# Window attention: v comes out with two windows' tokens on the partitions, and four copies deal the heads to the halves

## The reference

```
L0: window attention, windows of 8x8 tokens (4 per sample), 12 heads of 8 channels
    qkv = x_w @ qkv_w.T + qkv_b;  softmax(q k^T * scale + bias) v;  proj
L1: shifted window attention, the same windows after a roll by 4, 12 heads of 32 channels
    q, k, v = split(x_s @ w_qkv);  softmax(q k^T * scale + pos + masks) v;  @ w_out + b_out
L2: depthwise 3x3 convolution and a pointwise one, with weights rounded to -1, 0, 1
L3: attention with rounded activations ("spikes"), without softmax
```

## Time and profile before

| | us |
|---|---|
| median of 3 runs | 438.77 (437.97 to 439.72) |
| profiled execution | 439.99 |
| its span, first to last instruction | 438.1 |
| PE busy | 382.5 |
| DVE busy | 320.0 |
| ACT busy | 246.3 |
| POOL busy | 197.1 |
| v products (L736), PE busy, L1 and L0 | 26.4 and 11.1 |
| v copies (L923), DVE busy | 46.8 |

### The profile page before, as it was taken

The page is one execution under the profiler, slowest core; times in us unless marked ns, Lnnn a source line. Parts: engine busy times, 40 slices in busy tenths (PEclk is TensorE's granted clock), DMA queues, the critical chain, the costliest instruction groups (busy, mean ns, idle before and its releaser), DMA issues.

```text
span 438.1 us, 13521 instructions
## 1 busy us (share of the span) xinstructions
PE 382.5 (87%) x4971; PEld 282.5 (64%) x4971; DVE 320.0 (73%) x730; ACT 246.3 (56%) x554; POOL 197.1 (45%) x319
## 2 busy tenths in 40 slices
PE   0178599999999999999999999999999999858773
PEld 0168377888888787777777777777777533325441
DVE  0488288777787867878777777777878679965783
ACT  0010366878778675665666666666566455457871
POOL 8202056675666754445444444444544352442341
PEclk9999999999999999999999999999999999997996
DMA  8900000000000000000000000000000000000111
GB/s 290 166 9 1 0 4 1 4 0 0 0 0 0 3 2 3 2 1 1 2 3 1 0 0 0 0 0 1 1 2 3 1 0 0 1 0 18 39 37 54
DMA packets 8520, 7.15 MB, mean 16 GB/s; under 512 B 5058, under 2 KB 8130, under 8 KB 8354
## 3 DMA queue, kind: packets, MB, share of 16 engines
q1 hardware_dynamic: 3984, 5.26, 4.1%
q10 hardware_dynamic: 4498, 1.38, 1.8%
HBM read 5.06 MB, written 1.57 MB: 15 GB/s over the span
## 4 chain that ended last, share of the span: by engine, by line
PE 63%; DVE 16%; issue 9%; POOL 4%; DMA 3%; ACT 3%; DVEq 0%; POOLq 0%; ACTq 0%
PE bank L726 12%; PE bank L760 12%; PE bank L789 11%; PE bank L769 9%; PE bank L736 6%; DVE conv L1238 5%; PE bank L833 4%; PE bank L818 3%; DMA table<-in_L_conv_rpb_table 3%; POOL y_out L1437 2%; PE bank L555 2%; DVE stats L584 2%; DVE row_max L961 2%; PE bank L835 1%; PE bank L1346 1%
## 5 line engine op out<-in xcount | busy, mean ns | idle before, releaser
L999 POOL TENSOR_TENSOR probs<-probs,row_max 128x384 f32<-128x384 f32 x128 | 105.5, 830 | 128.4 <-DVE row_max L961 127.7
L957 DVE TENSOR_TENSOR probs<-bank,bias 128x384 f32<-128x384 f32 x128 | 65.4, 552 | 56.6 <-PE bank L760 56.4
L860 ACT ACTIVATE probsT<-bank 128x384 f32<-128x384 f32 x128 | 61.2, 492 | 63.7 <-PE bank L769 63.7
L961 DVE TENSOR_REDUCE row_max<-probs 128x6 f32<-128x384 f32 x128 | 68.2, 545 | 1.0
L769 PE MATMUL bank<-cst,probs 128*128 128x128 f32 x384 | 62.6, 280 | 0.0
L760 PE MATMUL bank<-k,q 64*64 64x128 f32 x1536 | 58.0, 282 | 3.7 <-ACT k L907 1.9
L789 PE MATMUL bank<-v,probsT 128*64 128x18 f32 (+1 forms) x1536 | 57.7, 219 | 1.2 <-DVE headsN L986 0.8
L760 PEld LDWEIGHTS bank<-k,q 64*64 64x64 f32 x1536 | 42.4, 135 | 25.3 <-issue 24.3
L789 PEld LDWEIGHTS bank<-v,probsT 128*64 128x64 f32 x1536 | 50.1, 137 | 12.6 <-issue 11.7
L923 DVE COPY v<-bank 64x384 f32<-64x384 f32 (+1 forms) x96 | 46.8, 487 | 9.6 <-PE bank L736 7.2
L769 PEld LDWEIGHTS bank<-cst,probs 128*128 128x128 f32 x384 | 44.4, 140 | 10.9 <-issue 5.0
(11 more groups left out here) (137 smaller groups left out, 581.4 us busy)
## 6 DMA issues: line engine op xcount, KB each, us to landing
rel_bc<-in_L_conv_rel_index SPq DMA_DIRECT2D x1, 2048.0 KB, 8.8
x<-in_x SPq DMA_DIRECT2D x4, 384.0 KB, 12.2
out_dram<-y_out SPq DMA_DIRECT2D x8, 192.0 KB, 2.1
w<-in_L_conv_w_qkv ACTq DMA_DIRECT2D x1, 432.0 KB, 4.9
cst<-in_consts ACTq DMA_DIRECT2D x1, 421.0 KB
p<-in_L_conv_w_out ACTq DMA_DIRECT2D x1, 144.0 KB, 4.7
pos<-in_L_conv_pos_emb SPq DMA_DIRECT2D x8, 2.0 KB
b_qk<-in_L_conv_qkv_b ACTq DMA_DIRECT2D x8, 0.1 KB, 6.8
```

The costliest lines, as they stand in the source:

```text
L860: nc.scalar.activation(probsT[w][:, :], ps_probsT[w % 2][:, 0:NP * 128], ACT.Exp).then_inc(L.s.probsT_sb, 1)
L957: nc.vector.tensor_tensor(out, scores, b, ALU.add).then_inc(L.s.biased, 1)
L961: nc.vector.tensor_reduce(row_max[w][:, :], probs[w][:, :, :], AX.X, ALU.max).then_inc(L.s.maxed, 1)
L999: nc.gpsimd.tensor_tensor(probs[w][:, :, :], probs[w][:, :, :], by_row(row_max[w]), ALU.subtract).then_inc(L.s.shifted, 1)
```

## The change

`pe_qkv` makes v for both windows of a pair at once: the stationary operand is 128 tokens of `xn` (a pair's two windows), the moving operand is the v weights of all 12 heads, and the output has a pair's tokens on the 128 partitions (window c on partitions c*64 on) and all heads along the columns. That is 1 matmul of 384 columns per v product in L1 and 2 of 96 columns in L0. `evac_v` gets a further index: each copy takes one window half c and one head h, so four per product, with 192 elements per partition in L1 (every second head's 32 columns) and 96 in L0; two of them go from one half of the partitions to the other. The plan's counts change with it. `dve_scores` puts two of the four copies ahead of the second maximum and two behind it; in L0 all four stand where the two stood.

```
--- before.py
+++ after.py
@@ -98,8 +98,8 @@
         self.n, self.hd = n, hd
         self.wide = hd == HD1
         self.slots = 1 if self.wide else NP
-        self.plan = [("qk", 0, 3), ("qk", 1, 3), ("v", 0, 2), ("qk", 2, 3), ("v", 1, 2)] if self.wide else \
-            [("q", 0, 3), ("k", 0, 2), ("v", 0, 2)]
+        self.plan = [("qk", 0, 3), ("qk", 1, 3), ("v", 0, 4), ("qk", 2, 3), ("v", 1, 4)] if self.wide else \
+            [("q", 0, 3), ("k", 0, 2), ("v", 0, 4)]
         self.qk_uses = 3 if self.wide else 2
         self.v_uses = 2 if self.wide else 1
 
@@ -728,13 +728,12 @@
                     last.then_inc(L.s.qk_ready, 1)
                     continue
 
-                n = NP * NU * L.hd
-                w_v = (w1[:, 2 * INNER:3 * INNER] if L.wide else w0T[:, 256:]).rearrange("i (g h d) -> i h g d", h=NH, d=L.hd)
-                windows = range(2 * j, 2 * j + 2) if L.wide else range(NW)
-                for at_, w in enumerate(windows):
-                    for h in range(NH):
-                        last = nc.tensor.matmul(o[h * WT:(h + 1) * WT, at_ * n:(at_ + 1) * n], xn[par][:, w * WT:(w + 1) * WT],
-                                                w_v[:, h], start=True, stop=True)
+                n = HEADS * L.hd
+                w_v = w1[:, 2 * INNER:3 * INNER] if L.wide else w0T[:, 256:]
+                pairs = (j,) if L.wide else range(2)
+                for at_, pair in enumerate(pairs):
+                    last = nc.tensor.matmul(o[:, at_ * n:(at_ + 1) * n], xn[par][:, pair * PAIR_COLS:(pair + 1) * PAIR_COLS], w_v,
+                                            start=True, stop=True)
                 last.then_inc(L.s.v_ready, 1)
 
         def pe_scores(pe, L, s, j):
@@ -911,22 +910,22 @@
                 return nc.scalar.activation(dst, src, ACT.Identity, scale=scale, bias=bias)
             return nc.vector.tensor_scalar(dst, src, scale, bias, ALU.mult, ALU.add)
 
-        def evac_v(eng, L, s, i, j, h):
+        def evac_v(eng, L, s, i, j, c, h):
 
 
             par = parity(s)
             b, _ = bank_of(L, par, i)
-            rows, n = slice(h * WT, (h + 1) * WT), (2 if L.wide else NW) * NP * NU
-            src = ps_qkv[b][rows, 0:n * L.hd].rearrange("k (g d) -> k g d", d=L.hd)
-            dst = (v1 if L.wide else v0)[par][rows, 2 * j:2 * j + (2 if L.wide else NW), :, h * (L.hd + 1):h * (L.hd + 1) + L.hd]
-            dst = dst.rearrange("k w g d -> k (w g) d")
+            pairs, first = (1, 2 * j) if L.wide else (2, 0)
+            src = ps_qkv[b][c * WT:(c + 1) * WT, 0:pairs * HEADS * L.hd].rearrange("k (w g h d) -> k w g h d", w=pairs, h=NH, d=L.hd)[:, :, :, h]
+            dst = (v1 if L.wide else v0)[par][h * WT:(h + 1) * WT, :, :, h * (L.hd + 1):h * (L.hd + 1) + L.hd]
+            dst = dst.rearrange("k (w c) g d -> k c w g d", c=2)[:, c, first // 2:first // 2 + pairs]
             return nc.scalar.copy(dst, src) if eng == "act" else nc.vector.tensor_copy(dst, src)
 
         def evacuate(eng, who, L, s, i, first=0, end=99):
 
             kind, j, _ = L.plan[i]
             if kind == "v":
-                todo = [lambda h=h: evac_v(who, L, s, i, j, h) for h in range(NH)]
+                todo = [lambda c=c, h=h: evac_v(who, L, s, i, j, c, h) for c in range(2) for h in range(NH)]
             else:
                 todo = []
                 if kind != "k":
@@ -968,8 +967,10 @@
             if heads:
                 dve_heads(dve, *heads, 1)
             elif between:
-                evacuate(dve, "dve", *between)
+                evacuate(dve, "dve", *between, 0, 2)
             dve_max(dve, L, s, 2 * j + 1)
+            if between:
+                evacuate(dve, "dve", *between, 2, 4)
 
         def dve_heads(dve, L, s, j):
```

## The result

The changed kernel took 452.23 us (median of 6 runs, 450.23 to 453.51), the kernel before 439.25 beside it: a ratio of 1.029 (95% interval 1.026 to 1.032). It is slower by 13.0 us; 6.0 were forecast, and 452.23 lies outside the range of 440.4 to 448.4. The profiled execution took 450.23 us (span 448.4). One run of a later variant, order_into, took 746.66 us in a much slower state and stands in no comparison.

What follows compares the result with a forecast made beforehand. TensorE, busy 382.5 of 438.1 us, was taken as the bound. L1 wait 4.5, norm samples 1.0 and 0.7, first copies 0.36, end 0.35, L0 product -0.9: +6.0 us, median 438.77 becoming 444.8; range 440.4 to 448.4.

Steps and rivals of the forecast that it cites:

- the forecast case: In L1, v copies delay the second q/k product; slower, 442 to 447.5 us with small variants; chance 0.70.
- Rival 3: VectorE's v copies are dearer, 0.45 us each; the wait becomes 0.8 us and the time 451 us; chance 0.10.
- Rival 2: VectorE ends the second v copies before 4.12 us, so every TensorE saving counts; 435.6 us; chance 0.05.
- Rival 1: Copies lose half their fixed part (278 ns); the wait shrinks to 0.10 us; 439.5 us; chance 0.15.
- +0.35 us per sample: L1: 0.40 us wait of the second q/k product, minus 0.05 for the first v product; 13 times, +4.5 us.
- the next copy overlaps a maximum by 0.07 as now: VectorE in L1: the copy behind the second maximum starts 0.07 us before that maximum ends, at 3.73 us.
- an end of the product 0.05 us later than now: L1's v product ends 0.05 us later, so the first copy starts at 2.49 us after the scores, not 2.44.
- I take -0.05 us: TensorE in L1: values to transposes changes by -0.05 us with the full-width v product, bounds 0 and -0.10.
- L0's product: TensorE in L0: two 96-column matmuls take 0.43 us, saving 0.07 us per sample; 13 times, -0.9 us.
- Norm samples: Samples with group-norm sums, where VectorE ends last: +0.5 us each, twice in L1 (+1.0); +0.36 each in L0 (+0.7).
- The end: End of L1: the values wait once for `headsN`, which comes behind the last copies; +0.35 us.
- No gain or loss from the clock is counted: TensorE's clock adds nothing: the loops are at its full level and its load hardly changes.

Runs made afterwards that it cites:

- order_into: Changed kernel with its four copies reordered: window half 0, heads 1 then 0, ahead of the second maximum, half 1 behind it; 448.19 us, ratio 1.022.
- the second profile: Second trace of the changed kernel, nothing edited; its runs took 451.96 us (median), ratio 1.029 to the kernel before.
- order_from: Changed kernel with its four copies reordered: head 1 of both window halves ahead of the second maximum, head 0 behind it; 448.32 us, ratio 1.022.
- Copies_alone: Kernel before with its old product, each of its two copies cut in two and placed around the second maximum; 447.47 us, ratio 1.018.
- product_alone: Kernel before with only the full-width v product, its own two copies kept, v's heads in wrong places; 440.75 us, ratio 1.003.
- product_behind: As product_alone, but a sample's first v product moved behind the transposes of window 0; 440.98 us, ratio 1.0035 to the kernel before.
- ahead: Changed kernel with all four copies of the second v product ahead of the second maximum; 444.97 us, ratio 1.013 to the kernel before.

## Why the prediction was wrong

**The mechanism was right, and the forecast case with it**: slower, by the wait of the second q/k product for the v copies, once per sample of L1's loop; L0's period all but unchanged (6.85 us, 6.80 said); 192 copies at 356 and 254 ns (351 and 250 said). Rival 3, dear copies, names a time near the one that came (451 against 452.23) and is refuted: not one copy was dear, and crossing halves is free. Rival 2's open path was seen only where the gate was taken away, and then the savings it counts on weren't there. Rival 1 fell with the copies' durations.

**The step that failed is the term "+0.35 us per sample"**: it is 0.69 (5.83 - 5.18 and 5.66 - 5.61). 13 x 0.34 = 4.4 us of the 7.0 by which the forecast fell short. The product of L0 makes 0.6 more, and the longer stretch at half rate 1.2 if the second profile stands for the median run, which is not shown. Some 0.8 are left without an owner. The parts of the 0.34:
- *"the next copy overlaps a maximum by 0.07 as now"*: 0.10 us too little. It starts 0.03 after it; order_into and order_from move the overlap from place to place and show why. The earlier trace rows held the warning: the second maximum there begins 0.04 after the copies while the first copy overlaps the first maximum. I read that as a property of the operations; it is one of the partitions.
- *"an end of the product 0.05 us later than now"*: the first copy starts at 2.62 instead of the 2.49 said, 0.13 us. It no longer follows the maximum but waits for the product, which ends later by about 0.2. Copies_alone, with the old product, still has 2.44.
- *"I take -0.05 us" for a product*: it costs +0.05, shown by product_alone in both halves. Off by 0.10 for v0, where nothing covers it. The change of shape ahead of the product is as I said (values to product 0.86 us), but a product that follows it takes 0.75 us and not 0.64; product_behind shows 0.10 of that to come from its place, and the rows put it down to a weight load that nothing hides. I had set that at nothing.
- Small ends in the copies' spacing: 0.03.

The Trainium skill has the rule for the first of these, and I didn't weigh it. Page "VectorE: DVE Perf Modes", section "Two Vector instructions with no wait between them": an instruction is held until all earlier ones have finished when the quadrant (32 partitions) in which its input or output starts differs from that of the last read of that memory or of the last output into it. The runs agree with it in every pair of copies and maxima shown here. The price, 0.10 us each time (0.03 after the end instead of 0.07 ahead of it), is theirs, not the page's. With it the gate opens at 4.51 + 0.10 = 4.61 us, and the term is 0.45.

**L0's product.** 0.07 us less per sample was said; the period went from 6.87 to 6.85. Values to product is 0.81 and product to transposes 0.52 us (127.66 to 128.18), so 1.33 against 1.31, with 0.05 less in the transposes behind. So 0.6 of the 0.9 us of gain didn't come. The prediction left open what paces the product. By columns its estimate was 0.32 us, 0.42 with the 0.10 of the unhidden first load; by one load of 0.11 for each pass it is 0.54. The trace has 0.52, which speaks for the loads. By the Trainium skill's page "TensorE: Matmul & The Clock Gate", section "LDWEIGHTS (loading the stationary operand)", four loads of 107 ns take 0.43 us, and with about 0.10 for the first load that gives an estimate of 0.53. The trace agrees with it.

**The terms that held.** Norm samples in L1: 0.5 each said, 0.56 and 0.55 measured (6.65 and 6.64 against 6.09). In L0: 0.36 each said, 0.32 and 0.42 measured. The end: 0.35 said, TensorE's wait for `headsN` grew by 0.5.

**The start.** Said was 0.36 us for the first sample's copies, which TensorE does wait for (0.43 at 55.91). Not said was that TensorE is at half its rate there in both kernels, and that the end of that stretch changes from execution to execution. "No gain or loss from the clock is counted", with the loops at full level, left the program's two ends out. The clock records of the traces begin with the full level, 2.4 GHz, at 55.30 us in the profile after, at 61.77 in the second one, at 58.18 and 58.39 in the two of the kernel before. The matmuls change from the longer to the shorter durations at just these times. TensorE was busy without a break from the first scores to the change in the profile after (3.33 us) and in the first one of the kernel before (6.68), and 9.60 of 9.97 us in the second profile. Against the kernel before, the stretch gave back 0.6 us in the first profile after and cost 1.2 in the second. What decides when the clock rises stays open: with the same instructions on TensorE, the second interval from scores to scores was 2.54 us after, 3.87 in the second profile, 3.36 in order_into and 3.64 in order_from.

**Behind L1's last scores** the code is the same in all kernels but took from 103.2 (order_into) to 104.8 us (ahead). The granted clock is at its half level, 1.2 GHz, for 8.2 us of it in order_into and for 15.4 in ahead, and TensorE is busy for 81.6 us there and for 83.5. So the clock is behind most of this spread, and likely behind much of the 2 us by which runs of one kernel differ. None of it is work of the change. In the kernel before it fell at 392.7 us, after TensorE had been busy for 8.36 of 12.7 us (19.14 of 20 just ahead of those).

## What to carry to other kernels

A gate with 0.49 us of slack is priced by placing every instruction ahead of it one after the other. Each pair's overlap or gap is a term of its own, here 0.10 us against the 0.15 us of a copy's fixed part: look in the trace for pairs with the same start partitions, not for pairs of the same operations. When matmuls of one shape follow those of another, whoever comes first pays for the change (here 0.10 us more than among its like); replacing the eight passes of each L1 product by two gained nothing there. And the cheap remedy for a gate is to take work out from in front of it: another place in the order gave 7.0 us back, and another engine made even the kernel before 2.9 us faster, where the product alone cost 1.0.

## What the runs showed of the hardware

- VectorE overlaps a copy or maximum with the one ahead of it by 0.07 to 0.08 us, or leaves 0.03 between them, by the partitions at which their inputs and outputs start. Changing only the order of four copies moved 0.10 to 0.12 us per sample.
- A copy from one half of the partitions to the other takes what a straight one takes (356 ns for 64x192, 0.73 to 0.75 us a pair).
- A 384-column product takes 0.75 us start to start behind 64-wide matmuls and 0.65 among 128-wide ones.
```profile
57.00:58.40 1.40, 1.40 (x25) 1.07 (x25) 0.65 (x2) 1.01 (x2) 1.14 (x2) 1.00 0.04 12
```

```profile
57.06:58.00 0.94, 0.94 (x25) 0.77 (x26) 0.79 (x3) 0.85 (x2) 0.55 (x1) 1.00 0.00 0
```

- ScalarE copies 64x384 from PSUM in 0.48 us, VectorE in 0.55.
